# A gated mixture-of-experts layer on one core: four small reorderings between VectorE, ScalarE, GpSimd and the weight loads

## The reference

```
def _L0_xattn_ref(hidden_states, token_ids, Wg, Wu, Wd):
    expert_ids = jnp.minimum(clip(token_ids) // 6250, 3)
    for e in range(4):
        g = jax.nn.silu(jnp.einsum('bsd,fd->bsf', hidden_states, Wg[e]))
        u = jnp.einsum('bsd,fd->bsf', hidden_states, Wu[e])
        y = jnp.einsum('bsf,df->bsd', g * u, Wd[e])
        out = jnp.where((expert_ids == e)[..., None], y, out)

def _L0_ffn_ref(x, gate_W, W1, b1, W2, b2):        # D_FF = 352, N_EXPERTS = 6, TOP_K = 2
    gate_probs = jax.nn.softmax(jnp.einsum('bd,ed->be', x.mean(axis=1), gate_W), axis=-1)
    topk_vals, topk_idx = jax.lax.top_k(gate_probs, TOP_K)
    topk_vals = topk_vals / topk_vals.sum(axis=-1, keepdims=True)
    h = gelu(jnp.einsum('bsd,bkdf->bksf', x, W1[topk_idx]) + b1[topk_idx][:, :, None, :])
    eo = jnp.einsum('bksf,bkfd->bksd', h, W2[topk_idx]) + b2[topk_idx][:, :, None, :]
    return jnp.einsum('bk,bksd->bsd', topk_vals, eo)

x = x + jnp.tanh(g_xattn[0]) * _L0_xattn_ref(_layernorm(x), ids, ctx_2048, ctx_2048, ctx_2048)
x = x + jnp.tanh(g_ffn[0]) * _L0_ffn_ref(_layernorm(x), gate_W, W1, b1, W2, b2)
```

## Time and profile before

| | |
|---|---|
| median of 3 runs | 277.35 us (277.03 to 277.98) |
| the profiled execution | 278.45 us |
| its span, first to last instruction | 276.6 us |
| busy, share of the span: PE, DVE, ACT, POOL | 97%, 80%, 52%, 33% |
| granted TensorE clock | 1.0 throughout |
| DMA moved | 40.25 MB, mean 145 GB/s |

### The profile page before, as it was taken

The page is one execution under the profiler, slowest core; times in us unless marked ns, Lnnn a source line. Parts: engine busy times, 40 slices in busy tenths (PEclk is TensorE's granted clock), DMA queues, the critical chain, the costliest instruction groups (busy, mean ns, idle before and its releaser), DMA issues.

```text
span 276.6 us, 4459 instructions
## 1 busy us (share of the span) xinstructions
PE 267.1 (97%) x1352; PEld 217.6 (79%) x1352; DVE 220.6 (80%) x508; ACT 145.0 (52%) x213; POOL 91.5 (33%) x124
## 2 busy tenths in 40 slices
PE   8989999998999999999999998999999899999995
PEld 7878888876888888878788876887778677888783
DVE  8798978879888899678897759998697976778074
ACT  4745332267667766764367125787258933544020
POOL 5565167547666566354233010050101301000000
PEclk9999999999999999999999999999999999999999
DMA  6880035265657976334951717995199803950004
GB/s 201 299 262 4 2 88 167 91 139 118 128 120 143 275 171 131 76 76 141 279 174 43 250 54 227 236 263 171 35 294 170 246 0 95 294 203 0 2 0 152
DMA packets 45282, 40.25 MB, mean 145 GB/s; under 512 B 25256, under 2 KB 33710, under 8 KB 45260
## 3 DMA queue, kind: packets, MB, share of 16 engines
q1 hardware_dynamic: 42048, 29.83, 41.3%
q0 software_dynamic: 3040, 9.98, 12.0%
q10 hardware_dynamic: 172, 0.15, 0.2%
HBM read 25.52 MB, written 9.19 MB: 125 GB/s over the span
## 4 chain that ended last, share of the span: by engine, by line
PE 75%; DVE 10%; DMA 4%; issue 4%; ACT 4%; POOL 2%; SPq 1%; DVEq 0%; ACTq 0%; POOLq 0%
PE bank L1312 32%; PE bank L1286 10%; PE bank L1288 10%; PE bank L1287 10%; PE bank L1303 3%; PE bank L1364 3%; DMA w_raw<-in_L_ffn_W 2%; DMA raw_ctx<-in_ctx 2%; PE bank L1509 1%; DVE ctx_hi L962 1%; PE bank L1510 1%; POOL expo L590 1%; DVE x_odd L971 1%; DVE x_even L971 1%; PE bank L1294 1%
## 5 line engine op out<-in xcount | busy, mean ns | idle before, releaser
L1286 PE MATMUL bank<-w_lo,ctx_hi 128*128 128x512 f32 x80 | 31.7, 396 | 1.3 <-DVE ctx_lo L963 1.3
L1288 PE MATMUL bank<-w_hi,ctx_lo 128*128 128x512 f32 x80 | 31.2, 390 | 0.0
L1287 PE MATMUL bank<-w_hi,ctx_hi 128*128 128x512 f32 x80 | 31.1, 389 | 0.0
L1176 ACT ACTIVATE act<-bank,tables 128x512 f32<-128x512 f32 x16 | 11.0, 687 | 35.9 <-PE bank L1288 33.8
L1052 ACT ACTIVATE aT_hi<-bank 128x512 fp32r<-128x512 f32 x18 | 10.8, 597 | 25.4 <-PE bank L1303 22.9
L546 POOL DMA_INDIRECT x_scratch<-x_ring,put_rows x17 | 22.4, 1318 | 4.9 <-POOL x_ring L545 4.4
L1169 ACT ACTIVATE w_hi<-w_raw 128x512 fp32r<-128x512 f32 (+3 forms) x22 | 20.9, 975 | 5.9 <-DMA w_raw<-in_L_ffn_W 5.9
L1312 PE MATMUL bank<-ctx_hi,hT_hi 128*128 (+1 forms) x80 | 23.4, 414 | 0.4 <-ACT hT_hi L1047 0.4
L1286 PE MATMUL bank<-ctx_lo,w_hi 128*128 128x512 f32 x60 | 23.6, 393 | 0.0
L1287 PE MATMUL bank<-ctx_hi,w_hi 128*128 128x512 f32 x60 | 23.4, 390 | 0.0
L1288 PE MATMUL bank<-ctx_hi,w_lo 128*128 128x512 f32 x60 | 23.4, 389 | 0.0
(11 more groups left out here) (236 smaller groups left out, 642.0 us busy)
## 6 DMA issues: line engine op xcount, KB each, us to landing
raw_ctx<-in_ctx SPq DMA_DIRECT2D x4, 1024.0 KB, 7.6
w_raw<-in_L_ffn_W SPq DMA_DIRECT2D x8, 512.0 KB
x_even<-x_scratch SPq DMA_DIRECT2D x8, 257.0 KB, 4.3
w_raw<-in_L_ffn_W SPq DMA_DIRECT2D x8, 256.0 KB
w_raw<-in_L_ffn_W SPq DMA_DIRECT2D x4, 448.0 KB, 3.5
out<-x_even SPq DMA_DIRECT2D x7, 256.0 KB, 2.4
w_raw<-in_L_ffn_W SPq DMA_DIRECT2D x4, 384.0 KB
x_odd<-x_scratch SPq DMA_DIRECT2D x4, 257.0 KB, 3.5
```

The costliest lines, as they stand in the source:

```text
L1176: sc.activation(act[:, c % 2, :], hid_ps[k % 2][:, :], ACT.Gelu, bias=b1_of(s, c, slice(0, P), chosen[s])).then_inc(gelu_done, 1)
L1286: pe.matmul(dst, s_hi, m_lo, start=first, stop=False)
L1287: pe.matmul(dst, s_hi, m_hi, start=False, stop=False)
L1288: return pe.matmul(dst, s_lo, m_hi, start=False, stop=last)
```

## The change

Five places move; no instruction is added or taken away, but for one wait.

```
@@ load_experts, SyncE
+                sp.dma_start(part_of(second, 0), w1_cols(two, MB, MB + P)).then_inc(w1_here[1], 16)
+                sp.dma_start(rest_of(second, 0, P + LW), w1_cols(two, MB + P, F2)).then_inc(w1_rest_here[1], 16)
                 for e, rows in ((one, (64, 65, 96)), (two, (66, 67, 97))):
                     for row in rows:
                         sp.dma_start(b2_rows[row:row + 1, :], b2[bass.ds(e, 1), :]).then_inc(w2_here[1], 16)
-                sp.dma_start(part_of(second, 0), w1_cols(two, MB, MB + P)).then_inc(w1_here[1], 16)
-                sp.dma_start(rest_of(second, 0, P + LW), w1_cols(two, MB + P, F2)).then_inc(w1_rest_here[1], 16)
@@ GpSimd, rows
-                ahead_of = j + AHEAD + (j > TURNED - AHEAD)
+                ahead_of = j + AHEAD + (j >= TURNED - AHEAD)
...
-                if j == TURNED - AHEAD:
+                if j == TURNED - AHEAD - 1:
                     inverse_root(ahead_of + 1)
@@ join_first, GpSimd
                 pool.wait_ge(words_turned[0], 16 * (b - 1))
+                wait_primed(pool, a2_ready, 2 * FC * (b - 1) + 2)
@@ VectorE, rows
                 a_low(j - 1)
+                if j == TURNED - 2:
+                    add(j - 2, y_ps)
+                    normalise(TURNED)
+                    rows_statistics(j + 3)
+                    up(j)
+                    normalise(j + 3)
+                    h_low(j + 1)
+                    statistics(j - 2)
+                    continue
...
                     h_low(j + 1)
-                    if j == TURNED - 2:
-                        rows_statistics(j + 3)
-                        normalise(j + 3)
+                    if j == TURNED - 3:
+                        rows_statistics(TURNED)
@@ batch, VectorE
                     scale_logits(b + 1)
+                if not joined_ahead:
+                    split_low(b, 1, 2)
+                if more:
                     choose(b + 1)
                     mixing(b + 1)
-                if not joined_ahead:
-                    split_low(b, 1, 2)
@@ tile_step, ScalarE
                 a_high(j - 1)
+                if j == TURNED - 2:
+                    part_row(TURNED)
...
                     h_high(j + 1)
-                if j == TURNED - 2:
-                    part_row(TURNED)
```

## The result

The changed kernel takes 276.24 us (median of 7 runs, 275.40 to 276.40) against 277.35 (7 runs, 276.81 to 277.98): ratio 0.9947, interval 0.993 to 0.9965. The interval lies clear of 1, so the kernel is faster, but the predicted range ended at 275.9, and about half of the 3.0 us is missing. A second session, with both kernels again, gave 275.43 (274.69 to 275.76) against 277.18, ratio 0.9944 (0.993 to 0.9958). The two medians of the first session are 1.1 us apart, those of the second 1.75; both ratios say 1.5 to 1.6, and I take 1.5 us.

What follows compares the result with a forecast made beforehand. TensorE is busy nearly throughout, so only its stops can give time back. Gains 1.35 (rows), 0.23 (low halves) and 1.43 (batch 2) sum to 3.0 us, taking the median from 277.35 to 274.3, range 272.9 to 275.9.

Steps and rivals of the forecast that it cites:

- all 1.43 is gained: Batch 2, second weighing: earlier cast and copies moved behind that weighing remove TensorE's whole stop of 1.43 us.
- the copies' part, 0.84: Batch 2: GpSimd's two copies lengthen the weighings by 0.84 us, which goes with the copies behind the second weighing.
- Bias rows amid the weights: Batches 1 and 2: weights issued ahead of six bias rows close a DMA queue hole, so GpSimd's cast starts sooner.
- my 0.77: Batch 2: closing the DMA hole brings GpSimd's cast 0.77 us sooner; if only the cast moved, 0.77 gained at most.
- rival 5: Slower: SyncE's transfers share DMA engines, so weights issued sooner delay the first half's last pieces; up to 279.6, chance 0.05.
- The copies in their new place: Copies beside VectorE's low halves cost 0.84 us there, just covered before the third weighing; uncovered, 0.3 in each batch.
- From there the order is the old one: After tile 6's turn in the rows, the remaining order was taken as unchanged, following the rows' gain.
- my 1.35: Rows: moving tile 7's work a step sooner gains 1.35 us of TensorE's two stops of 1.67 together.
- My walk up to the statistics of tile 3: Rows: step times in the new order, with the statistics of tile 3 ending near 57.5, some 3 us later.
- a stop of over 0.5 us at a place of its own: Sign that the prediction is wrong: a TensorE stop over 0.5 us at a place it did not name.
- Low halves in the wait for the powers: Batch 0: low-half subtractions moved ahead of the choice hold GpSimd's expo; gain 0.23 us, bounds 0.2 and 1.14.
- Face value, 1.14: Batch 0: the moved subtraction is wholly hidden in VectorE's wait, without the read-interface rule, gaining 1.14 us.

Runs made afterwards that it cites:

- e9: Kernel before, with GpSimd's cast in batches 1 and 2 made to wait for the batch's first gelu: 278.39 us, ratio 1.0034.
- e8: Changed kernel with 128x1536 subtraction behind batch 0's first weighing and w2 subtraction in the x_odd wait, but old SyncE order and join: 274.61 us, 0.9905 to kernel before.
- e10: Changed kernel, with GpSimd's cast in batches 1 and 2 made to wait for the first gelu: 276.06 us, ratio 0.9952 to the kernel before.
- after: The changed kernel itself with all edits, first session's profile: median 276.24 us, ratio 0.9947 to the kernel before; profiled execution 276.33 us.
- e2: Kernel before with only the new SyncE order of weights and bias rows and GpSimd's wait ahead of the join: 276.74 us, ratio 0.999.
- e3: Changed kernel with VectorE's 128x1536 subtraction of batch 0 moved behind its first weighing, freeing tile 18's power: 275.16 us, ratio 0.9933 to kernel before.
- e11: Changed kernel with batch 0's w2 subtraction back behind the mixing: 275.51 us, ratio 0.9936 to the kernel before.
- e5: Changed kernel with batch 0's 128x1536 subtraction behind the first weighing and its w2 subtraction in VectorE's x_odd wait: 274.31 us, ratio 0.9901 to kernel before.
- before_again: The kernel before, unchanged, profiled a second time: median 277.19 us over 12 runs, profiled execution 277.09.

## Why the prediction was wrong, point by point

**The step that failed first: "all 1.43 is gained", taken from a profile and laid on a median.** The working of the stop was right for the copies' part, 0.84 (`e9` makes 0.85 of it at will in batch 2, `e8` has 0.71 with weights in time, and `e10` has none); that the rest of the 1.43, when the weights are late, goes as I had it was not made at will, but the profiles of `after`, `e2`, `e3` and `e11` had batch 2's second piece as late (6.6 to 7.3 us from the issue, 7.0 in the execution of the earlier trace rows) and have no stop in batch 2. Its frequency was wrong. It stood in one profiled execution, and that took 1.1 us more than the median and 0.5 more than the slowest of the runs then known. I wrote this distance down and carried it along as a constant, when most of it was the very stop that I subtracted. Four profiles have the join in its old place and no late cast: the stop is in batch 2 of one, in batch 1 of another (`e8`, 0.71), and in neither batch of two. Of the 67 runs of the kernel before between the others, nine took over 278.0. In the median the two edits are worth 0.1 to 0.3: 0.24 in `e2`, 0.3 between `e5` and `e8` (0.1 by their ratios), neither told from nothing by its interval. About 1.2 of the missing 1.5 is here, and no rival of mine covered it.

**Bias rows amid the weights:** the hole narrowed, as I had it, but no run shows time gained by it. From 6 to 7 us after the issue of batch 2's first weights, where the old order has its hole, the DMA engines moved 125 to 174 GB/s in six profiles with that order (146 in the mean) and 184 to 264 in eight with the new one (236). From the issue to the start of the cast it took, with the old order, 15.36 (the execution of the earlier trace rows), 13.38, 13.56, 13.77 and 13.31; with the new, 14.03, 13.19, 13.82, 13.87, 12.92, 12.40 and 14.63. Those times hang first on when the second piece comes. Where ScalarE began it within 5.5 us of the issue, the cast came after 13.5 in the mean with the old order and 12.8 with the new, 0.7 sooner, near my 0.77; where it came after 6.6 or more, 15.36 in one profile and 14.1 in the mean of four. But the second piece was late, by over 6 us, in four of eight profiles with the new order and in two of six with the old; in batch 1 in four of eight and one of six. That may be chance, or a cost of the new order, as in rival 5: these profiles don't decide it.

**The copies in their new place** lengthen the low halves by 1.0 (0.93 and 1.19 us instead of 0.42 and 0.69, in `after`), where I had 0.84; TensorE doesn't stop behind them, so they are covered as I had said.

**The step that failed second: "From there the order is the old one".** The rows gave 1.57, more than my 1.35 (`up(6)` ended at 62.4, I had 62.65 to 63.0; GpSimd's root of tile 9 began at 60.65 where I had 60.9 to 61.2). My walk up to the statistics of tile 3 came out within 0.1 at each step. But I let the gain run to the end unhindered, and there is a chain beside TensorE with no slack: last power, scatter, its report, loads, h. In the profile before, h was finished a moment ahead of TensorE. The prediction named a stop of over 0.5 us at a place of its own as what would make it wrong, and this is one. Moved 1.6 sooner TensorE meets a wait that varies with the DMA: 1.31, 0 (under 0.25), 0.58, 0.62, 0.90 and 0 in six profiles with the new rows and the held power, 0.57 in the mean; 0, 0.42, 0, 0 and 0.74 with the old rows, 0.23 in the mean. Net 0.3 us, an estimate from eleven profiles. With the power free it is 0 in three of three. What the DMA's times hang on, 4.1 to 5.1 us from issue to report for the same scatter behind the held power, stays open.

**Low halves in the wait for the powers:** right in its mechanism. The subtraction ran from 161.79 to 163.00 and `expo` ended 1.24 behind it (I had 1.36 − 0.14 = 1.22), held as in the single case of the earlier trace rows; the gain is 0.1 where I had 0.23, from one profile each with and without the edit. The Trainium skill, "SBUF — State Buffer", section "Who interferes with whom", says that the first of the two keeps the other out; the traces agree both ways, with 2.27 against 1.36 for GpSimd here, and 1.83 against 0.75 for the low half of VectorE's weighing in `e10`, where the cast began first. Face value, 1.14, falls.

**Sum.** 1.57 − 0.3 + (0.1 to 0.3) + 0.1 = 1.5 to 1.7, measured 1.5 by either ratio. Against the prediction the terms differ by +0.2 for the rows, −0.3 for the wait at h2, −0.1 for the low halves and −1.2 for batch 2. The close match is in part luck: the terms come from single profiles and from medians that don't stand clear of noise. The range failed because its lower and upper ends were made of the trace's mechanisms only, and not of how often each would occur.

## What to carry to other kernels

A stop in one profile is worth its size only if it stands in most executions: where the profiled one lies above all other runs, look for the stop of that size, and take a second profile before counting on it. A gain ahead in the program runs only to the next place where TensorE meets a chain that isn't its own; list for each such place how close the other side arrives today. And a small GpSimd instruction on such a chain should not be issued just behind a VectorE instruction that reads two tensors from SBUF: in this kernel freeing two of these gave a further 1.1 us, when the VectorE instruction could be moved to where VectorE had time.

## What the runs showed of the hardware

A DMA's report varies from one execution to the next by as much as the effects looked for: the same scatter took 4.1 to 5.1 us from issue to report in the eleven profiles in which GpSimd took 1.37 or 1.38 to issue it (3.8 to 4.0 in the three in which that took 1.03), and from the issue of batch 2's first weights to ScalarE's start on the second piece it was 4.8 to 5.5 us in eight profiles and 6.1 to 7.3 in six. GpSimd's two copies of 128x512 words take 1.45 us where VectorE is mostly idle (`before_again`) and 1.9 to 2.1 beside its two-input instructions.
